# Causal attention with an ALiBi bias: one order of a head for all engines, or one for each

## The reference, cut to what matters

```python
def _layernorm(x): ...                      # x is 2 x 2048 x 512
xn = _layernorm(x, axis=-1)
q, k, v = (proj(Wq, bq), proj(Wk, bk), proj(Wv, bv))       # 2 x 16 heads x 2048 x 32
scores = jnp.einsum('bhqd,bhkd->bhqk', q, k) / jnp.sqrt(jnp.float32(HD))
scores = scores + _alibi_slopes(H)[None, :, None, None] * distances[None, None, None, :]
scores = jnp.where(causal, scores, jnp.finfo(scores.dtype).min)
attn = jax.nn.softmax(scores, axis=-1)
ctx = jnp.einsum('bhqk,bhkd->bhqd', attn, v)
attn_out = ctx.transpose(0, 2, 1, 3).reshape(b, s, d) @ Wo + bo
return x + attn_out + ffn(xn)               # ffn: 8 experts, the best 2 of each token
```

## Time and profile before

| | us |
|---|---|
| median of 3 runs | 1971.01 |
| lowest, highest | 1967.87, 1974.89 |
| span of the profiled execution | 1970.9 |
| of it the 30 periods of heads, 368.0 to 1439.1 | 1071.1 |
| TensorE busy in the span | 1897.6 |
| DVE, ScalarE, POOL busy | 1501.2, 1400.8, 1372.3 |

### The profile page before, as it was taken

How to read it: one execution, slowest core, us unless ns; L and a number is a source line. 1 busy time by engine, 2 the same in 40 slices (tenths; PEclk the granted TensorE clock), 3 DMA queues, 4 the chain that set the end, 5 groups by cost and what they waited for, 6 DMA issues and landing times. The chain is left out here.

```text
span 1970.9 us, 39142 instructions
## 1 busy us (share of the span) xinstructions
PE 1897.6 (96%) x8656; PEld 1425.0 (72%) x8657; DVE 1501.2 (76%) x3466; ACT 1400.8 (71%) x2728; POOL 1372.3 (70%) x1183
## 2 busy tenths in 40 slices
PE   6999999999999999999999999999998989999997
PEld 5787777676767777777677776776756767887876
DVE  6454566888989989899899898898966965666654
ACT  4333322998999989999999899998973335555554
POOL 4111113898988989889889898898948846666664
PEclk9999999999999999999999999999999999999998
DMA  8577758242242432423324224243226766656554
GB/s 268 193 260 258 272 179 283 75 114 64 73 104 61 97 80 63 113 62 81 96 62 108 69 71 106 61 96 81 62 72 183 252 197 118 104 103 104 104 99 66
DMA packets 119241, 242.13 MB, mean 123 GB/s; under 512 B 17632, under 2 KB 54368, under 8 KB 112896
## 3 DMA queue, kind: packets, MB, share of 16 engines
q1 hardware_dynamic: 101120, 205.84, 36.0%
q0 software_dynamic: 18080, 35.81, 10.3%
HBM read 139.28 MB, written 104.21 MB: 124 GB/s over the span
## 5 line engine op out<-in xcount | busy, mean ns | idle before, releaser
L1173 POOL TENSOR_TENSOR probs_lo<-probs,probs_hi 128x512 fp32r<-128x512 f32 x781 | 984.1, 1291 | 158.6 <-ACT probs L1208 156.7
L1207 ACT ACTIVATE probs_hi<-s_ps 128x512 fp32r<-128x512 f32 x905 | 602.0, 665 | 84.3 <-DVE s_ps L1280 80.2
L1208 ACT ACTIVATE probs<-s_ps 128x512 f32<-128x512 f32 x964 | 613.3, 670 | 9.8 <-DVE s_ps L1280 6.4
L1259 DVE TENSOR_REDUCE m_part<-m_ps 128x1 f32<-128x512 f32 x744 | 491.1, 685 | 9.5 <-PE m_ps L1500 5.9
L1516 PE MATMUL s_ps<-q_st,k_st 100*128 100x512 f32 (+3 forms) x880 | 327.9, 413 | 16.5 <-ACT probs L1208 11.8
L1500 PE MATMUL m_ps<-k_st,q_st 98*128 98x512 f32 (+2 forms) x840 | 282.0, 377 | 0.3 <-DVE m_part L1256 0.3
L1535 PE MATMUL o_ps<-probs_hi,v_split 128*96 128x512 f32 (+3 forms) x720 | 266.8, 380 | 1.7 <-POOL probs_lo L1173 1.7
L1536 PE MATMUL o_ps<-probs_lo,v_split 128*96 128x512 f32 (+3 forms) x720 | 259.2, 363 | 0.0
L1256 DVE CUSTOM_DVE_ANT_0 m_ps<-m_ps,mask_row 128x128 f32<-128x128 f32 x496 | 242.0, 498 | 22.5 <-PE m_ps L1500 16.3
L1516 PEld LDWEIGHTS s_ps<-q_st,k_st 100*128 100x128 f32 x880 | 161.5, 190 | 103.0 <-ACT probs L1208 37.9
L621 POOL TENSOR_TENSOR v_rows<-v_raw,v_rows 128x512 fp32r<-128x512 f32 x32 | 41.2, 1291 | 229.4 <-ACT v_rows L677 229.4
(11 more groups left out here) (236 smaller groups left out, 3658.2 us busy)
## 6 DMA issues: line engine op xcount, KB each, us to landing
v_d<-v_rows SPq DMA_DIRECT2D x7, 3072.0 KB, 9.4
v_split<-v_d SPq DMA_DIRECT2D x22, 768.0 KB, 8.5
k_st<-k_hi_d SPq DMA_DIRECT2D x44, 256.0 KB
q_st<-q_hi_d SPq DMA_DIRECT2D x44, 256.0 KB
xn_d<-xs SPq DMA_DIRECT2D x8, 1024.0 KB, 11.7
q_hi_d<-qk_hi SPq DMA_DIRECT2D x32, 256.0 KB, 8.0
q_lo_d<-qk_lo SPq DMA_DIRECT2D x32, 256.0 KB, 7.9
k_hi_d<-qk_hi SPq DMA_DIRECT2D x32, 256.0 KB, 3.5
```

Source lines behind the costliest of these rows:

```text
L1173: nc.gpsimd.tensor_tensor(*low_operands(u), ALU.subtract).then_inc(lo_ready_pool, 1)
L1207: nc.scalar.activation(probs_hi[:, P_SLOT[u]], scores, ACT.Exp, scale=SCALE)
L1208: nc.scalar.activation(scores if kind == "Q" else probs[:, P_SLOT[u]], scores, ACT.Exp, scale=SCALE).then_inc(p_ready, 1)
L1259: V.tensor_reduce(top, scores, AX.X, ALU.max).then_inc(m_taken, 1)
```

## The change

Each engine gets an order of its own, `ORDERS`, with its own letters and its own count of steps that belong to the head before (`BACK`): 7 V on TensorE, 1 O on ScalarE, 2 O on DVE, 4 L on POOL. SP follows DVE's order. `KIND` now has 26 P, 5 Q and 3 W (units 1, 3 and 26; they were 2, 9, 18, 26 and 29). In DVE's order S stands only for units with a mask. The slot loads are issued behind the fourth O of the head before (`(kind, u, back) == ("O", QCS - 1, 1)`) instead of behind the head's own second. The wait on `m_placed` stands before the scores of unit 0, behind three M and two V, instead of at the head of the pass.

```diff
-KIND = "PPWPPPPPPWPPPPQPPPWPPQPQPPWPPWQPPP"
+KIND = "PWPWPPPQPQPPPQPPPPPPPQPPPPWPPPQPPP"
-ORDER = ("SMMMVVVMVMMVLSSMVMLLSMVMMVOVSLMSMVSLSMLMLVSMSMVSLMLMLVMMOVSMSSVMMSVMVMDOSLMVLLSVSMVSVMSMVSMMVSMVMSLD"
-         "LVSLMLLVMDLSMVSMMSSVMSVLSVXWVSLVLLDSOVSVLLS")
-BACK = {'V': 8, 'L': 4, 'O': 1}
+ORDERS = {"PE": ("MVMVMSMVSMSVMMSMVSVMSVSMSMVSVMMMSVVSSVMMMVSMVMSVMSMVMSVMVSSMMSVMMSVVSMMSMVMSMVSVVMMSVSMSMVMSMVSMSMVS"
+              "VVSWVSVVS"),
+          "ACT": ("SSSSSSOSSSSOSSSSSSOSSSSSSSSSSSSSSSSOSS"),
+          "DVE": ("MMMSMSMMSOMMMMSMSOMDMMDMMMMOMMDMMMSMSMMMSMMMMMDOMMMMMMMMXWDSS"),
+          "POOL": ("LLLLLLLLLLLLLLLLLLLLLLLLLL"),}
+BACK = {("PE", "V"): 7, ("ACT", "O"): 1, ("DVE", "O"): 2, ("POOL", "L"): 4}
...
-    for kind in ORDER:
-        at = seen[kind] - BACK.get(kind, 0)
+    for kind in ORDERS[engine]:
+        at = seen[kind] - BACK.get((engine, kind), 0)
...
-ATTEND = attend_order()
+ATTEND = {engine: attend_order(engine) for engine in ORDERS}
...
+LAST_ORDER = last_order()
+LAST_ATTEND = {engine: [token for token in LAST_ORDER if not token[2] or token in ATTEND[engine]] for engine in ORDERS}
...
-                for kind, u, back in ATTEND if maxima else LAST_ATTEND:
+                for kind, u, back in (ATTEND if maxima else LAST_ATTEND)["DVE"]:
                     if kind == "O" and (before or not back):
                         store_context(n - back, u)
 
-                    if kind == "O" and u == 1:
+                    if (kind, u, back) == ("O", QCS - 1, 1):
                         if load_ahead:
...
-                pe.wait_ge(m_placed, 32 * (n + 1))
                 if maxima:
                     pe.wait_ge(st_loaded[r1], 16 * ST_DMAS * st_round)
-                for kind, u, back in ATTEND if maxima else LAST_ATTEND:
+                for kind, u, back in (ATTEND if maxima else LAST_ATTEND)["PE"]:
...
+                    if (kind, u) == ("S", 0):
+                        pe.wait_ge(m_placed, 32 * (n + 1))
```

More of the change, by code:

```diff
@@ L136, with attend_order @@
 S_BANK = [u % S_BUFS for u in range(NS - 1)] + [1]
[L139 to L143, removed]
+def attend_order(engine):
+    units = {"S": [u for u in range(NS) if engine != "DVE" or s_diagonals(u)], "M": list(range(NM)), "V": list(range(NS)),
+             "X": [0], "W": [0], "L": [u for u in range(NS) if KIND[u] == "P"],
+             "D": [u for u in range(NS) if KIND[u] == "Q"], "O": list(range(S // CH))}
     order, seen = [], collections.Counter()
-    for kind in ORDER:
-        at = seen[kind] - BACK.get(kind, 0)
+    for kind in ORDERS[engine]:
+        at = seen[kind] - BACK.get((engine, kind), 0)
         order.append((kind, units[kind][at], int(at < 0)))
         seen[kind] += 1
-    assert all(seen[kind] == len(units[kind]) for kind in units)
+    assert all(seen[kind] == len(units[kind]) for kind in seen)
     return order
-ATTEND = attend_order()
+ATTEND = {engine: attend_order(engine) for engine in ORDERS}
 LAST_KIND = "".join("PW"[u in LAST_WHOLE] for u in range(NS))
@@ L159, in last_order @@
 def last_order():
[L161 to L164, removed]
+    waiting = {k: sorted({(k, u, 1) for order in ATTEND.values() for kind, u, back in order if kind == k and back})
+               for k in "VLDO"}
+    due = [*range(3 - len(waiting["O"]), 3)] + [u + LAST_LAG + 3 for u in LAST_UNIT]
     waiting["V"] += [("V", u, 0) for u in range(NS)]
@@ L167, in last_order @@
     waiting["O"] += [("O", u, 0) for u in range(S // CH)]
-    due = [2] + [u + LAST_LAG + 3 for u in LAST_UNIT]
-    order, late = [], BACK["V"]
+    order = waiting["D"]
     for u in range(NS + LAST_LAG + 4):
@@ L184, in last_order @@
             due.pop(0)
-    assert not any(waiting.values())
+    assert not any(waiting[kind] for kind in "VLO")
     return order
-LAST_ATTEND = last_order()
+LAST_ORDER = last_order()
+LAST_ATTEND = {engine: [token for token in LAST_ORDER if not token[2] or token in ATTEND[engine]] for engine in ORDERS}
 LOOPS = (NH - 2) // HEADS_RING
@@ L1175, in step_n @@
             def step_n(n, before=True):
-                for kind, u, back in LAST_ATTEND if is_last(n) else ATTEND:
+                for kind, u, back in (LAST_ATTEND if is_last(n) else ATTEND)["POOL"]:
                     if kind == "L" and (before or not back):
@@ L1225, in step_n @@
             def step_n(n, before=True):
-                for kind, u, back in LAST_ATTEND if is_last(n) else ATTEND:
+                for kind, u, back in (LAST_ATTEND if is_last(n) else ATTEND)["ACT"]:
                     if kind == "S":
```

## The result

The changed kernel takes 1925.17 us in the median (1923.01 to 1926.88, 4 runs), the kernel before in the same comparison 1969.81 us. The ratio is 0.9768, with a 95% interval of 0.9747 to 0.9789: faster by 2.3%, 45 us. The forecast was 1928 us within 1908 to 1956.

A forecast was written before the change was run, and what follows sets the result against it. TensorE was taken as the bound. Per head 0.80 + 0.36 + 0.65 - 0.4 = 1.4 us saved; thirty periods make 42 us, the first head about 1: 1970.9 - 43 = 1928 us, range 1908 to 1956.

The forecast's parts named there:

- A: The forecast case: TensorE keeps the bound, the turn is healed, 34.0 to 34.6 us a head, 1919 to 1937 us; chance 0.52.
- (1): Two whole units fewer on TensorE, each swap saving 0.40 us: 0.80 us a head gained.
- (2): Extra low parts on POOL and DVE, two more exponentials on ScalarE: directly costed at nothing, ScalarE's rest shrinking to 0.5 to 1.3 us.
- (3): Turn between heads: the new order removes TensorE's late starts there, 0.65 + 0.36 = 1.01 us a head.
- the 0.65: At the turn, unit 33's scores start 0.65 us late, waiting for ScalarE's weights; the new order covers this.
- The 0.36: At the turn, TensorE idles 0.36 us before the next head's first scores, waiting for `m_placed`; taken as gone.
- (4): New small waits of TensorE for score and maxima slots: 0.4 us a head lost, bounds 0 and 1.0.
- (5): Slot loads issued some 12 us earlier, ahead of the first chunk's store; slot read a head later: costed at nothing.
- B: Rival: only the columns pay, waits move into the head's body; 34.9 to 35.2 us a head, 1946 to 1955 us; chance 0.28.
- D: Rival: slower, ScalarE sets the length, its mask rests exceeding 1.85 us a head; 36.65 us a head, 1999 us; chance 0.07.

The follow-up runs named there:

- e1: Changed kernel with five whole units again instead of three (units 9 and 18 whole), new orders kept: 1935.88 us, ratio 0.9817 to the kernel before.
- g2: Kernel before with its one order, only the kinds changed to three whole units (units 9 and 29 in parts): 1985.73 us, ratio 1.0069.
- f3: Changed kernel with DVE's reductions of three maxima tiles reading 128 of 512 columns: 1923.22 us, ratio 0.9756 to the kernel before.
- f4: Changed kernel with POOL's low part of unit 16 taking 128 of 512 columns from head 1 on: 1925.66 us, ratio 0.9768 to the kernel before.
- f2: Changed kernel with ScalarE's second exponentials of units 12, 19 and 28 taking 128 of 512 columns: 1918.19 us, ratio 0.9731 to the kernel before.
- e2: Changed kernel with the wait on `m_placed` back at the head of the pass, ahead of M0: 1959.05 us, ratio 0.9936 to the kernel before.
- e4: Changed kernel with DVE's addition of the third chunk's sums back before the masks of units 32 and 33: 1953.38 us, ratio 0.9909.
- e3: Changed kernel with the slot loads back behind the head's own second sums: 2129.51 us, ratio 1.0811 to the kernel before.
- f1: Changed kernel without TensorE's low products of units 5, 12, 22 and 28: 1916.54 us, ratio 0.9729 to the kernel before.

## Why the prediction was right, and where its steps were not

- **The size, A.** 34.3 us a head and 1928 us were forecast, 34.29 and 1925.17 measured; outside of the periods 1 us was forecast, and the profiled span shows 5.8, of which 2.2 in the last head, forecast as nothing, and 3.1 behind the attention. The signs named for it came: transposes 34.29 us apart, POOL busy 95% of the loop, ScalarE idle for 0.74 us a head, and no idle time in TensorE's rows before unit 33 and unit 0.
- **(1) Two whole units fewer, 0.80.** The instructions cost what was said, but the step to the path was mis-sized: in the new orders the kinds are worth 0.33 (e1), and in the old one, placed as in g2, they cost 0.52. The 131 ns a matmul of the Trainium skill ("TensorE: Matmul & The Clock Gate", "Back-to-back issue gap") is not seen in any run here: pairs still start 0.23 apart at a granted clock of 1.00.
- **(2) Cover on ScalarE.** "Costed at nothing" holds for POOL and DVE (f3, f4) and not for ScalarE: 0.96 us of it is worth 0.20 a head (f2).
- **(3) The turn, 1.01.** The place is right, and the 0.65 is: unit 33's scores come 0.05 us late now. The 0.36 was misread. It is not the wait for `m_placed` and not a loss of every head: it stands at one turn in three, and at the others unit 33 to S0 takes the 0.39 us that unit 33 to M0 takes now without this wait. In the mean of 30 turns, unit 33's start to the next matmul fell from 0.56 to 0.44 us, late transfers included: 0.12 a head for the 0.36. That the orders give 1.08 all the same, with as many whole units as before (e1), and so near to 1.01, is in part luck: with 0.60 at unit 33 and 0.12 behind it, some 0.4 of it lie elsewhere in the head, and no run says where. Put back one by one, the wait costs 1.07 (e2) and DVE's sums 0.85 (e4). Together that is more than 1.08: in the new order each step relies on the others.
- **(4) New waits, 0.4.** The sum came out because this term, set against the columns' 0.80, leaves 0.40 where 0.33 was measured. I had chosen it between the bounds 0 and 1.0 and as a term of its own, so this too is partly luck; e1 suggests that it is the price of the kinds, ScalarE's 0.95 us.
- **(5) The loads, nothing.** The cost was right for the change as made, but the reason was wrong: they are due at the next turn, not a head later. In the changed kernel all ten are issued by 1003.37, 16 us before the next transpose (1019.37); in e3 the last of a slot goes out at 1023.63, 1.5 us before it, and the kernel is 8% slower than before.
- **Rivals.** B's head of 34.9 to 35.2 did not come, though its mechanism, columns swallowed by waits, is what e1 shows in part. D's sign was seen only in g2, the kinds without the orders: there ScalarE waits some 2.2 us a head for masks, over the 1.85 that D asked for, and the kernel is slower. The rule of the Trainium skill beside it ("Perfetto Trace Analysis", "Identifying the Most-Contended Engine"), which names ScalarE, is borne out by half: in the changed kernel ScalarE's microsecond is worth as much as TensorE's within the scatter (0.20 in f2, 0.17 in f1), not more. ScalarE rests 0.73 us a head for a mask now, well under the 1.85 from which D would decide.

## What to carry to other kernels

When several engines are within a few per cent of each other, read the distance between starts at the point where all of them meet (here the turn of a head): an engine's own busy share names the bound, but the gain lies in what stands in front of whom there. Read several such points before pricing one: a gap that comes once in a pass of a loop of three heads is worth a third of what it shows. One order shared by all engines ties unrelated steps together; one order for each lets a mask go ahead of sums, but then check for each transfer which step of the next pass reads it first, since moving a trigger moves its loads too. And before cutting work on the fullest engine, cut a similar amount on its neighbour as well, each alone and both together: it shows within three runs what each is worth.

## What the runs showed of the hardware

Two transfers of 8 KB behind ten loads of up to 768 KB took 6.9 us to land in the median, although they are small, while the DMA engines were 97% busy (e3). In the changed kernel, where the DMA engines are 3% busy behind the issue at 985.92, they take 1.8. Whether they waited for their place in SP's queue or for a share of the engines, the run doesn't separate. And a stall costs more than its length: after a stretch of 5 us in which TensorE was busy 2.45 us, its granted clock was 0.54 (with a second wait of 1.30 us in that stretch) and 0.78 in the two stretches that followed, with matmuls 0.43 us apart at the lower level, and 1.00 again after that (e3).
